# Turning the rows of eight more units through DRAM, and taking the turned probabilities' rests ahead of the 32x32 turns

## The reference, cut to what matters

```
q, k, v = x @ Wq.T, x @ Wk.T, x @ Wv.T        # 32 query heads, 8 key heads, head size 128
q, k = rmsnorm(q) * q_norm_w, rmsnorm(k) * k_norm_w
scores = q k^T / sqrt(128) + slope(head) * (key - query), masked where key > query
out = softmax(scores) v ; result = out @ Wo.T
```

## Time and profile before

| | |
|---|---|
| median of 3 runs | 1202.82 us (1202.43 to 1203.24) |
| the profiled execution, its own time | 1202.77 us |
| its span in the profile | 1201.5 us |
| PE busy | 1183.3 us, 98% of the span |
| DVE, ACT, POOL busy | 886.9 us (74%), 757.2 us (63%), 668.2 us (56%) |
| DMA | 125.24 MB, mean 104 GB/s |

### The profile page before, as it was taken

The page is one execution under the profiler, slowest core; times in us unless marked ns, Lnnn a source line. Parts: engine busy times, 40 slices in busy tenths (PEclk is TensorE's granted clock), DMA queues, the critical chain, the costliest instruction groups (busy, mean ns, idle before and its releaser), DMA issues.

```text
span 1201.5 us, 18492 instructions
## 1 busy us (share of the span) xinstructions
PE 1183.3 (98%) x6128; PEld 1035.9 (86%) x6128; DVE 886.9 (74%) x2071; ACT 757.2 (63%) x1764; POOL 668.2 (56%) x538
## 2 busy tenths in 40 slices
PE   6999999999999999999999999999999999999999
PEld 5888888899998899899898899899898888888887
DVE  7876666687787687887887877877877878655555
ACT  4554443347677768778778778778777865544442
POOL 4796662545686625824834834834834344965540
PEclk9999999999999999999999999999999999999999
DMA  6152332213234145244244244244244120211101
GB/s 239 41 171 99 109 107 105 88 53 110 81 131 130 56 145 150 88 145 149 87 148 143 90 149 142 92 147 144 92 144 138 50 70 1 88 54 53 53 18 70
DMA packets 69310, 125.24 MB, mean 104 GB/s; under 512 B 8096, under 2 KB 33600, under 8 KB 68192
## 3 DMA queue, kind: packets, MB, share of 16 engines
q1 hardware_dynamic: 68976, 123.76, 32.1%
q10 hardware_dynamic: 240, 0.30, 0.1%
HBM read 78.42 MB, written 45.61 MB: 103 GB/s over the span
## 4 chain that ended last, share of the span: by engine, by line
PE 80%; POOL 6%; DVE 4%; ACT 4%; issue 3%; DMA 2%; SPq 1%; POOLq 0%; DVEq 0%; ACTq 0%
PE bank L406 18%; PE bank L408 18%; PE bank L407 18%; PE bank L518 4%; PE bank L513 4%; PE bank L512 4%; PE bank L720 4%; PE bank L739 2%; PE bank L734 2%; PE bank L735 2%; POOL rows L1926 1%; ACT prob L1125 1%; PE bank L434 1%; ACT prob L1134 1%; DMA turned_rows<-row_turns 1%
## 5 line engine op out<-in xcount | busy, mean ns | idle before, releaser
L1125 ACT ACTIVATE prob<-prob,neg_top 128x128 f32<-128x128 f32 (+3 forms) x256 | 141.5, 556 | 72.2 <-DVE neg_top L1608 67.5
L1926 POOL TENSOR_TENSOR rows<-rows,row_root_y 128x640 f32<-128x640 f32 x64 | 81.8, 1278 | 175.6 <-DVE row_root_y L1279 174.4
L1920 POOL TENSOR_TENSOR square<-rows 128x640 f32<-128x640 f32 x64 | 79.9, 1265 | 133.0 <-DVE rows L1651 108.7
L1794 POOL TENSOR_TENSOR w_l_late<-raw_late,w_h_late 128x512 fp32r<-128x512 f32 (+1 forms) x59 | 91.7, 1568 | 71.7 <-ACT w_h_late L856 71.5
L1134 ACT ACTIVATE prob<-prob,inverse 128x128 f32<-128x128 f32 (+3 forms) x252 | 121.0, 555 | 1.7 <-DVE inverse L1613 1.7
L1355 DVE SCALAR_TENSOR_TENSOR x_rows<-bank,x_rows 128x512 f32<-128x512 f32 x111 | 74.9, 687 | 44.3 <-PE bank L518 44.3
L1626 DVE TENSOR_TENSOR probT_l<-bank,probT_h 128x512 fp32r<-128x512 f32 x160 | 100.4, 675 | 3.9 <-ACT probT_h L1140 3.6
L1140 ACT CAST probT_h<-bank 128x512 fp32r<-128x512 f32 x160 | 84.5, 595 | 27.0 <-PE bank L720 26.9
L408 PE MATMUL bank<-o_h,oT_l 128*128 128x512 f32 x256 | 100.9, 394 | 0.0
L407 PE MATMUL bank<-o_l,oT_h 128*128 128x512 f32 x256 | 100.6, 393 | 0.0
L406 PE MATMUL bank<-o_h,oT_h 128*128 128x512 f32 x256 | 100.4, 392 | 0.2 <-DVE oT_l L1632 0.2
(11 more groups left out here) (246 smaller groups left out, 3815.6 us busy)
## 6 DMA issues: line engine op xcount, KB each, us to landing
x_ring<-x_between SPq DMA_DIRECT2D x64, 256.0 KB, 2.7
row_turns<-row_blocks SPq DMA_DIRECT2D x48, 320.0 KB, 2.2
turned_rows<-row_turns SPq DMA_DIRECT2D x192, 80.0 KB, 2.1
x_between<-x_ring SPq DMA_DIRECT2D x56, 256.0 KB, 2.1
raw_late<-w_qkv SPq DMA_DIRECT2D x16, 768.0 KB, 4.9
raw_early<-ffn_w SPq DMA_DIRECT2D x21, 512.0 KB, 4.1
scaled<-raw_early SPq DMA_DIRECT2D x21, 512.0 KB, 2.7
raw_late<-scaled SPq DMA_DIRECT2D x21, 512.0 KB, 3.7
```

Of the source, the lines that this page charges most:

```text
L1125: last = act.activation(p, p, ACT.Exp, bias=neg_top[:, h:h + 1], scale=-1.0, accum_out=total[:, h:h + 1])
L1794: return pool.tensor_tensor(lo, raw, hi.bitcast(F32), ALU.subtract)
L1926: pool.tensor_tensor(row, row, by, ALU.mult).then_inc(rows_normed, 1)
```

## The change

Three edits. First, only unit 13 stays plain among units 4 to 60: units 6, 10, 14, 21, 29, 37, 45 and 53 go through DRAM like the others (56 blocked units). Second, slots 20, 28, 36, 44 and 52 become `rows_between` slots. Their turn of unit n + 1 keeps its place on DVE and ACT, but ACT and POOL split only the first of the three weight blocks before the sum of product 6, or before `values_lo`, and the other two after. Third, DVE makes the rests of the turned probabilities ahead of the 32x32 turn of unit n + 2 in all slots with t = 0 (n = 4, 8, ..., 56), and in `rows_between` slots ahead of `project_out(n - 1)` as well. In odd slots under 12, `block_rows(n + 2)` moves behind `turn_rows(n + 1)`.

```diff
-PLAIN_ROWS = 6, 10, 13, 14, *range(21, UNITS, B * TB)
+PLAIN_ROWS = (13,)
...
         def rows_early(n):
 
-            return no_turn(n) and in_halves(n)
+            return no_turn(n) and n % (B * TB) == 0
+
+        def rows_between(n):
+
+            return no_turn(n) and n % (B * TB) == TB
...
-                if no_turn(n) and n % 2 == 0 and not rows_early(n):
+                if no_turn(n) and n % 2 == 0 and not rows_early(n) and not rows_between(n):
                     turn_rows(n + 1)
...
-                if not rows_first and not (no_turn(n) and n % 2 == 0):
+                if not rows_first and (rows_between(n) or not (no_turn(n) and n % 2 == 0)):
                     turn_rows(n + 1)
...
+                elif rows_between(n):
+                    split_qkv(g + 1, *splits[:1])
+                    take_sum(ahead, 6)
                 elif not behind:
                     split_qkv(g + 1, *splits)
...
-                if paired(ahead) and not half_behind:
+                if paired(ahead) and not half_behind and not rows_between(n):
                     take_sum(ahead, 6) if n % 2 == 0 else take_left(ahead - 1)
                 if n:
                     turn_probabilities(n)
-                if half_behind:
+                if half_behind or rows_between(n):
                     split_qkv(g + 1, *splits[1:])
...
-                if n % 2 and n + 2 in BLOCKED:
+                if paired(ahead) and n % 2 and n + 2 in BLOCKED:
                     block_rows(n + 2)
-                turn_first = n in (0, FIRST_PAIRED - LEAD) or no_turn(n) and n % 2 == 0
+                turn_first = n in (0, FIRST_PAIRED - LEAD) or no_turn(n) and n % 2 == 0 and not rows_between(n)
...
+                if not paired(ahead) and n % 2 and n + 2 in BLOCKED:
+                    block_rows(n + 2)
                 if n == 0:
                     turn_probabilities(n)
                 if ahead < FIRST_PAIRED:
                     values_lo(ahead)
+                if turn_between:
+                    turn_probabilities(n)
                 if n:
                     project_out(n - 1)
+                if in_halves(n) and not turn_between:
+                    turn_probabilities(n)
...
                 if n % 2 == 0 and n + 2 in BLOCKED:
                     block_rows(n + 2)
-                if n:
+                if n and not in_halves(n):
                     turn_probabilities(n)
...
+                splits = list(QKV_WHEN[g + 1 >= SEVEN_FROM].get(at, ())) if g < HKV - 1 else []
+                if rows_between(n) and splits:
+                    split_qkv(g + 1, splits.pop(0))
                 if n % 2 == 0 and paired(n + 2):
                     values_lo(n + 2)
...
-                if g < HKV - 1:
-                    split_qkv(g + 1, *QKV_WHEN[g + 1 >= SEVEN_FROM].get(at, ()))
+                split_qkv(g + 1, *splits)
```

## The result

The changed kernel takes 1209.0 us (median of 5 runs, 1207.81 to 1212.56), the kernel before in the same session 1202.88 (1202.43 to 1203.39). The ratio is 1.0054, 95% interval 1.0041 to 1.0066: 6.1 us slower by the medians, where 0.9 faster was forecast. The profiled execution is the slowest of the five, 1212.56 us with a span of 1211.3, and so shows 9.8 us of loss where the medians show 6.1.

What follows compares the result with a forecast made beforehand. PE, busy 98%, was taken as the bound, with five 0.88 us waits for DVE's rests; what PE waits for next limits gains. Terms -1.8 + 1.8 - 0.9 = -0.9 against 1202.77 gave 1201.9 us, range 1198.9 to 1205.2.

Steps and rivals of the forecast that it cites:

- part 4: Units 6, 10 and 14 through DRAM: -0.9 us, bounds -1.6 and +1.0.
- The fourth rival: DVE held by POOL in rests of rows through DRAM, costing 2 x 1.1 in units 6 and 10: 1204.1 us, chance 0.10.
- Part 3: Rests ahead in six slots like 24: squares 0.88 later, scores of units like 18 late, +1.8 us.
- Part 2: Rests ahead in five slots like 20: PE's 0.88 wait goes, but unit 22's rests limit the gain to -1.8 us.
- Part 1: Transposes off PE: 0.54 us shorter per unit, 4.3 us for eight units, of PE's path alone.
- The third: Rival: DRAM turn starts every sixth score once store plus fetch exceed about 5.9 us; six slots +5.3, 1206.7 us, chance 0.15.
- The first: Rival: PE takes all of it, scores of unit 22 and its like not held; -8.7 us to 1194.1, chance 0.10.
- second: Rival: roots or DMAs come sooner in the attention; part 2 -3.0, part 3 +0.5, part 4 -1.2, 1199.1 us, chance 0.12.

Runs made afterwards that it cites:

- e3: Kernel before with units 6, 10, 14 through DRAM, rests ahead in slots 4, 8, 12, squares behind rests in odd slots under 12: 1207.7 us, ratio 1.0036.
- e9: Kernel before with units 6, 10 and 14 through DRAM and DVE's order unchanged: 1204.47 us, ratio 1.0011.
- e8: e3 with the squares of odd slots under 12 back ahead of the rests, as in the kernel before: 1205.34 us, ratio 1.0018.
- e5: Changed kernel with 128 already satisfied waits at PE's start, which move the instruction loads: 1206.97 us, ratio 1.0034.
- e13: Changed kernel with 192 already satisfied waits at PE's start: 1206.41 us, ratio 1.0030.
- e1: Kernel before with rests of the turned probabilities ahead of the squares in slots 16, 24, 32, 40, 48 and 56 only: 1203.61 us, ratio 1.0009.
- e12: Changed kernel without its early part: units 6, 10, 14 plain, slots under 16 in the order of before: 1204.44 us, ratio 1.0012.
- e11: e2 with 128 already satisfied waits at PE's start: 1201.88 us, ratio 0.9992.
- e2: Kernel before with units 21, 29, 37, 45, 53 through DRAM, the rows_between slots, and rests ahead only in those five slots: 1202.41 us, ratio 0.9997.
- e15: Kernel before with 192 already satisfied waits at PE's start: 1206.14 us, ratio 1.0028.

## Why the prediction was wrong

**The step that failed is part 4.** It gave units 6, 10 and 14 -0.9 us with bounds -1.6 and +1.0; e3 measured 5.0 us by the medians (4.3 by the ratio), of which 3.2 show in slots 4 to 13 of its profile. Three things were wrong in it:
- "the rests follow 1.6 later (556.11 to 557.72 in rows 7)". I took the duration from unit 26, far away in the trace, though the kernel before has seven rests of keys beside units 6 and 10, all 1.34 to 1.40 us. By them the rest ends at 328.5, not 327.4, against PE's wish of 327.5: 1.0 us lost for each against the wish, so about 0.5 over the kernel before. Slots 5 and 9 of the change are 0.52 and 0.57 longer. The fourth rival had this size ("2 x 1.1") and this mechanism, but as an accident with a chance of 0.10. It held for every rest of keys there but one (e9's of unit 10).
- The move of the squares in odd slots under 12 stood in the change and got no term at all. e8 shows it to be worth about 2.2 us of e3's loss by the ratios: squares of unit 7 behind the late rests of unit 6, and scores of units 7 and 11 late by 0.95 and 0.7 us. In the change a load met both of these stores (2.2 and 2.1 us after their start); with the same order and no load there, slot 6 lost nothing and slot 10 0.5 (e5, e13).
- Unit 14 was said to have 1 us in hand. After the change its scores start 0.10 us after its rest.

**Part 3 had the chain right and the size off.** It took +1.8 us from bounds +0.5 and +3.1. The profile of the change shows +4.8, e5 +1.8, e13 +0.8, e1 +0.4 and e12 -0.1. The chain squares, store, fetch, rests, scores is as told where the turn is long, and the point from which it decides, 5.9 us, is 6.0 in e13. "moved loads may meet the fetches instead" is just what happened, in six of six. The six slots lie near 90 us apart, with about four loads in between, and in the change the loads fell alike in all six; in the kernel before they met the stores of three, the fetch of one and nothing in two. Where they fall is not in the forecast at all, so that the middle value could come out (e5) or miss by 3 us, by luck. For the case without loads I had written 6 x 0.14 = 0.8. That was wrong too: it took the 0.88 us of the squares for 0.88 us of the rests, and e1 shows 0.93 and 0.36. Its four slots that met no long turn lost nothing, and e13's 0.79 is one turn that met a load.

**Part 2 had the mechanism right; its size also hangs on the loads.** It said -1.8 with bounds -0.8 and -3.0. The pairs gave -0.95 in the change, where four gave -1.68 and the fifth lost 0.74 with a load 3.9 us after its store. The same five slots gave -1.97 in e11 and -1.70 in e13, but -0.27 in e2, -0.22 in e5 and -0.13 in e12, outside the bounds. Unit 22's scores stand at 0.10 us from the rest, so the 1.42 us of PE's shorter path were indeed not to be had. Part 1's 0.54 us of PE did come out, as slot 5 of e9 shows (0.45).

**The rivals.** The third (the DRAM turn becomes the start of every sixth score) came true in the profile: +4.8 against its 5.3, with loads on all six fetches, which it had not named as its cause. The fourth came true in the early slots. Either alone would have ended at 1204 to 1207; the change took both, and I had made them exclusive. The first and second are refuted by unit 22's distance and by e2.

**What stays open.** Slot 51 of the change lost 1.5 us (e5's lost 1.0): ACT stood 2.00 us for the fetch of unit 52, and behind it in ACT's queue is the scaling of the probabilities that PE turns next, which then made PE wait three times. Slot 42 of e12 has the same 2.00 us of ACT and lost 1.2. That row was not tested by itself. Also open is why e9 is 1.3 us slower when its early slots are not, and how much of the 6.1 us belongs to loads: at 192 waits the two kernels' attentions are 0.7 us apart and their medians 0.3, so up to all of it may, but these are single profiles, and e15 has losses of its own in six late slots.

## What to carry to other kernels

Price a moved operation by the rows nearest to its new place, in the same stretch, not by the cleanest row of the trace: the same rest took 0.35 us or 1.40, depending on what POOL does there. When one step moves behind another that gets later, the two delays add (1.0 and 1.0 us came to 2.3), so ask of each edit in the diff, the small ones too, what it now stands behind. And before a transfer is put in front of PE with under 1 us in hand, look where the loads of instructions fall: here they met all six turns of one kind in the change and four of the six in the kernel before. Padding PE's program with satisfied waits is a cheap way to find out which part of a difference is theirs, if both kernels are padded alike and the padding's own cost at the start is taken off.

## What the runs showed of the hardware

A load of instructions, 16 KB and 0.9 to 1.4 us on one DMA engine, that meets the store or the fetches of a turn mostly lengthens it. Counted over all 17 profiles for units 18, 26, 34, 42, 50 and 58: store and fetch of 320 KB took 5.5 to 6.3 us in the 25 turns without a load and 6.15 to 7.1 in the 33 with one that began 2.5 to 4.6 us after the store. A store alone took 2.15 to 2.25 us without one and up to 3.6 with one at its start; units 7 and 11 of the change, with one at its end, 4.15 and 4.18. Satisfied waits that compute nothing moved the kernel before by -0.13% (128 of them) and +0.28% (192, of which most lies ahead of the attention in its profile).

DVE's rest of the keys, with two operands in SBUF, ends when POOL's instruction does (327.97 after 327.82) and takes 0.34 us where POOL is idle; so it was for all the rests of the 17 profiles (1.33 to 1.95 us beside a POOL instruction, 0.34 to 0.35 without). The squares, which read one operand in SBUF, were not held: those of unit 7 took 0.83 us (from 327.89), as anywhere else, though POOL had an instruction of 2.45 us from 327.78 on.
